# Two relational graph layers, gathered in slots of four chunks in place of eight

## The chip, the cores and the metric

The kernel runs on one core of one Trainium2 chip. The metric is the time of the whole kernel on the device, in microseconds (us), lower is better. Engines: PE (TensorE, matrix products), DVE (VectorE), ACT (ScalarE), POOL (GpSimd, here the engine that issues gathers), SP (which issues plain DMAs). They run side by side and wait for each other by semaphores.

## What is computed

3125 nodes with 128 features, 100,000 edges sorted by destination, each with one of 8 relations. A graph convolution of two layers, a layer norm, then a relational part of two layers and a second layer norm:

```
def _rgcn_layer(x, W, SW, b, src, dst, rel):
    xt = jnp.einsum('nd,rde->rne', x, W)
    msg = xt[rel, src]
    agg = jax.ops.segment_sum(msg, dst, num_segments=x.shape[0])
    return jax.nn.relu(agg + x @ SW + b)
x = _layernorm(x + _L0_gnn_ref(x, ...))
x = _layernorm(x + _L1_gnn_ref(x, ...))   # two _rgcn_layer
```

The change touches the two relational layers alone, which the kernel numbers 2 and 3.

## The kernel before

Nodes are padded to NP = 3200 (25 tiles of 128). Edges are taken in chunks of 128, 782 in all. With the sorted destinations, chunk c reaches a window of WIN = 64 nodes that begins BACK = 32 nodes ahead of node 4c.

**Two ways to add up.** Each relational layer splits its nodes. The first nodes (1280 in layer 2, 1536 in layer 3) are *summed*: counts of edges by destination, relation and source ("halves" of 32 nodes, 1.6 MB each, built on PE in strips, L1297, from one-hots that DVE makes, L1809 and L1812, copied by ACT, L929) are multiplied by the features, split into three bf16 parts (L1385). One pair of halves takes 75 products; two pairs make a quad of 128 nodes, which `end_quad` multiplies by the relation weights (L1432, L1435). DVE (layer 2, L1917) or ACT (layer 3, L982) copies the sums of a pair from PSUM before that. The other nodes are *gathered*: the rows x·W of all nodes and relations lie in a table in DRAM (`table_rel`), POOL gathers the 128 rows of a chunk by an indirect DMA (L798), and PE multiplies them by a one-hot of destinations (`add_message`, L1408) which DVE makes for a whole batch (`node_onehots`, L1925).

**Slots.** PE's program in a relational layer is written as a row of slots, and `Gathers` sets their number: one for each batch of CH = 8 chunks, 59 in layer 2 and 51 in layer 3. A slot holds a share of the counts and sum products (`Made` cuts 384 steps over all slots but the last two of layer 2; `spread_sums` deals the 1725 products of layer 3 over all but the last three) and the messages of its batch, spread evenly among the products. Ahead of the first message of a batch PE waits for the batch's one-hots (`node_hots`) and for all its rows (`got_rows`). At a slot's end PE does what came due in it: `end_quad`, and in layer 2 the turning of a finished tile and its rows for layer 3's table (`turn_tile`, L1445; `row_products`, L1449; the second row product follows in the middle of the next slot). ACT and DVE do their parts (L1004, L1007, L1014; L1933, L1938, L1944) in the same slots, SP stores the rows (L651), halves (L668) and results. One tile is begun in a slot at most (`tile_order`). In layer 3 a final norm follows by `turn_final` (L1517), ACT's L989 or L997, DVE's L1954 and L1961 to L1969.

**Buffers and pace.** Gathered rows have GATHERS = 6 buffers of 8 chunks (three in the memory of `node_id`, three in that of `acc`), one-hots ONEHOTS = 4 of 8 chunks. POOL may gather batch n once batch n - 6 was used, and is also paced: ahead of each two gathers of slot n it waits until PE has come as far in slot n - AHEAD (AHEAD = 2), in layer 2 by counted strips (`rstrip_counted`), in layer 3 by quarters of a slot's products (`quarter_summed`, four to a slot).

Of the kernel before, what the change touches and what calls it, by code (L numbers as in the profile page):

```python
# [4 lines left out]
N_NODES, D, R, CTX = 3125, 128, 8, 64  # L5
# [6 lines left out]
CH = BATCH // P  # L12
# [3 lines left out]
CHUNKS = -(-E // P)  # L16
# [46 lines left out]
BACK, WIN = 32, 64  # L63
GATHERS, ONEHOTS, HOTS, RINGS = 6, 4, 3, 4

AHEAD = 2
QUAD = 4 * HALF
# [31 lines left out]
class Gathers:  # L99
# [5 lines left out]
    def __init__(self, first_node):  # L105
        self.first_node = first_node
        self.first = (first_node - BACK) // PER_CHUNK + 1
        self.slots = -(-(CHUNKS - self.first) // CH)
        whole = NP - LAST_BLOCK
        self.blocks = [(a, min(a + BANK, whole)) for a in range(first_node, whole, BANK)] + [(whole, NP)]  # L110
        self.in_slot = [[] for _ in range(self.slots)]
        self.end_slot = []
        self.batch_end = {}
        slot = 0
        for q, (a, b) in enumerate(self.blocks):
            for c in range(self.first, CHUNKS):
                base = PER_CHUNK * c - BACK
                if base + WIN > a and base < b:
                    batch = (c - self.first) // CH
                    slot = max(slot, batch)  # L120
                    self.batch_end[batch] = (slot, len(self.in_slot[slot]))
                    self.in_slot[slot].append((c, max(a, base), min(b, base + WIN), q))
            self.end_slot.append(slot)
            slot = min(slot + 1, self.slots - 1)

    def chunks(self, batch):
        first = self.first + CH * batch
        return first, min(CH, CHUNKS - first)

# [88 lines left out]
def gnn_kernel(nc, x, src, dst, rel, ctx_in, W1, b1, W2, b2, Wg, bg, Wb, w1, sl1, rb1, w2, sl2, rb2, out):  # L218
# [8 lines left out]
    with ExitStack() as stack:  # L227
# [6 lines left out]
        raw = sb("raw", [P, 8, BATCH])  # L234
# [17 lines left out]
        node_id = sb("node_id", [P, NP + W])  # L252
# [18 lines left out]
        acc = sb("acc", [P, NP + W])  # L271
# [16 lines left out]
        def carve(at, n):  # L288
# [18 lines left out]
        half_pairs = [blocks[:, u, :].rearrange("p (h n) -> p h n", h=2) for u in range(2)]  # L307
        nodehot = raw[:, 5:7, :].rearrange("p a (u c w) -> p (a u) c w", u=2, c=CH)
        rest3 = raw[:, 7, 0:2 * P].rearrange("p (u n) -> p u n", u=2)
# [8 lines left out]
            + [edge_mem[:, 2 * EDGE_COLS:2 * EDGE_COLS + NP // 2].bitcast(bf16)]  # L318
        got = [m[:, u * CH * D:(u + 1) * CH * D].rearrange("p (c f) -> p c f", c=CH) for m in (node_id, acc) for u in range(3)]
        wg1, wg2, ws1, ws2 = (sb(n, [P, D]) for n in ("wg1", "wg2", "ws1", "ws2"))  # L320
# [51 lines left out]
        half_summed, half_copied, quarter_summed = sem("half_summed"), sem("half_copied"), sem("quarter_summed")  # L372
# [111 lines left out]
        for layer in (2, 3):  # L484
            for n in range(gathers[layer].slots):
                u = (first_batch[layer] + n) % GATHERS
# [237 lines left out]
        def _(pool):  # L724
# [42 lines left out]
            def rest_of(slow):  # L767
# [8 lines left out]
                if not slow:  # L776
                    pool.wait_ge(edges_copied, CH)
                    for layer in (2, 3):
# [5 lines left out]
                        for n in range(gathers[layer].slots):  # L784
# [5 lines left out]
                            for j in range(chunks):  # L790
# [4 lines left out]
                                if layer == 3 and j % 2 == 0 and n >= AHEAD and sums3[n - AHEAD]:  # L795
                                    pool.wait_ge(quarter_summed, 4 * (n - AHEAD) + j // 2 + 1)
                                    pool.nop(nofuse=True)
# [289 lines left out]
        def _(pe):  # L1087
# [119 lines left out]
            def rest_of(slow):  # L1207
# [184 lines left out]
                def add_message(layer, s, i):  # L1392
                    own = gathers[layer]
                    c, a, b, q = own.in_slot[s][i]
                    batch, j = (c - own.first) // CH, (c - own.first) % CH
                    m = first_batch[layer] + batch
                    start_, end_ = own.blocks[q]
                    if c == next(chunk for t in own.in_slot for chunk, _, _, block_ in t if block_ == q):
                        if first_block[layer] + q:
                            pe.wait_ge(gather_out, first_block[layer] + q)  # L1400
                        nc.tensor.matmul(ps[:, GATHER_BANK, 0:end_ - start_], layer_self[layer][:, :], layer_in[layer][:, start_:end_],
                                         start=True, stop=False)
                    if i == 0 or (own.in_slot[s][i - 1][0] - own.first) // CH != batch:
                        pe.wait_ge(node_hots, m + 1)
                        pe.wait_ge(got_rows[m % GATHERS], rows_until[m])
# [666 lines left out]
```

## Time and profile before

| | |
|---|---|
| median of 3 runs | 1827.04 us (1826.1 to 1836.43) |
| profiled execution | 1842.08 us |
| its span, first to last instruction | 1840.2 us |
| PE busy | 1562.5 us (85%) |
| DVE busy | 779.7 us (42%) |
| ACT busy | 520.8 us (28%) |
| POOL busy | 917.4 us (50%) |
| mean granted clock of PE | 0.949 of full |
| chain that ended last | PE 66%, DVE 14% |

PE's clock has two levels, 1.2 and 2.4 GHz; a granted clock of 0.83 in a stretch is a mean over both. The relational layers begin where POOL's first gather does, at 462 us, and layer 3's first gather is at 1231 us. Busy times overlap between engines, so what counts is where PE stands still, and what it then waits for.

### The profile page before, as it was taken

How to read it: one execution, taken by the hardware profiler on the slowest of the kernel's cores; microseconds unless marked ns; L12 is line 12 of the kernel's file. 1: busy time of each engine (PE TensorE's matmuls, PEld its weight loads, DVE VectorE, ACT ScalarE, POOL GpSimd, SP SyncE). 2: the span in 40 equal slices, each digit the busy share in tenths (PEclk: the TensorE clock that was granted, in tenths of full speed). 3: DMA queues.
4: the chain of work that ended last, by engine and by line, in shares of the span. 5: the costliest groups of instructions: out<-in, count | busy, mean ns of one | idle time of the engine just before them, and what ended most of it. 6: DMA issues, size and time to landing. Idle time of an engine off the chain costs nothing.

```text
span 1840.2 us, 25393 instructions
## 1 busy us (share of the span) xinstructions
PE 1562.5 (85%) x9744; PEld 949.8 (52%) x9744; DVE 779.7 (42%) x2390; ACT 520.8 (28%) x749; POOL 917.4 (50%) x931
## 2 busy tenths in 40 slices
PE   1379989998578889988899787898888998889986
PEld 1365554444355556555565455554555655556545
DVE  7999961337345555555465654530010010001102
ACT  0464520015234435444354543420000000000000
POOL 6500000000566566666666665646666666666665
PEclk9999999999789899999899998998999999989988
DMA  4312331534443444544455443325555355555441
GB/s 124 103 73 90 127 162 72 195 129 185 155 141 134 151 156 165 189 163 159 151 182 179 157 157 122 113 82 189 186 192 189 123 190 188 190 189 178 172 148 47
DMA packets 67473, 275.85 MB, mean 150 GB/s; under 512 B 19988, under 2 KB 25854, under 8 KB 54676
## 3 DMA queue, kind: packets, MB, share of 16 engines
q1 hardware_dynamic: 37940, 213.87, 30.1%
q0 software_dynamic: 29408, 60.29, 12.1%
q8 instruction: 81, 1.33, 0.3%
q14 instruction: 44, 0.36, 0.1%
HBM read 153.70 MB, written 120.38 MB: 149 GB/s over the span
## 4 chain that ended last, share of the span: by engine, by line
PE 66%; DVE 14%; another core or an unknown queue 6%; issue 6%; DMA 3%; POOL 2%; ACT 2%; POOLq 0%; DVEq 0%; ACTq 0%
PE ps L1385 34%; DVE hot_mem L1667 8%; PE ps L1408 8%; PE ps L1263 7%; PE ps L1297 7%; PE ps L1449 2%; PE ps L1435 2%; PE ps L1306 2%; ACT blocks L929 2%; DMA node_id<-table_rel,edges 1%; POOL node_id L798 1%; DMA acc<-table_rel,edges 1%; DVE hot_mem L1812 1%; POOL acc L798 1%
## 5 line engine op out<-in xcount | busy, mean ns | idle before, releaser
L798 POOL DMA_INDIRECT node_id<-table_rel,edges x445 | 439.0, 987 | 608.0 <-DMA table_rel<-node_id 358.3
L798 POOL DMA_INDIRECT acc<-table_rel,edges x429 | 419.3, 977 | 257.5 <-issue 113.2
L1385 PE MATMUL ps<-blocks,raw 128*128 128x512 f16 x1500 | 456.5, 393 | 15.5 <-DVE xn L1917 12.5
L929 ACT ACTIVATE blocks<-ps 128x800 f16<-128x800 f32 x384 | 315.6, 836 | 342.3 <-PE ps L1297 200.0
L1385 PE MATMUL ps<-blocks,dinv 128*128 128x512 f16 x1200 | 399.3, 395 | 13.5 <-issue 12.8
L1809 DVE TENSOR_SCALAR hot_mem<-cell_h,rel_cols 128x128 f16<-128x128 f16 x768 | 165.6, 268 | 265.9 <-PE ps L1297 152.9
L1297 PE MATMUL ps<-hot_mem 128*128 128x400 f16 x768 | 198.8, 344 | 68.0 <-ACT blocks L929 47.5
L1408 PEld LDWEIGHTS ps<-raw,node_id 128*128 128x128 f32 x996 | 193.8, 200 | 97.7 <-issue 38.9
L1385 PE MATMUL ps<-blocks,edges 128*128 128x512 f16 x600 | 236.8, 395 | 7.9 <-issue 7.6
L1408 PEld LDWEIGHTS ps<-raw,acc 128*128 128x128 f32 x962 | 183.7, 197 | 85.4 <-issue 31.0
L1812 DVE TENSOR_SCALAR hot_mem<-cell_h,rel_cols 128x400 f16<-128x400 f16 x768 | 224.8, 333 | 0.0
L1385 PEld LDWEIGHTS ps<-blocks,raw 128*128 128x128 bf16 x1500 | 164.4, 116 | 110.7 <-issue 35.1
L1408 PE MATMUL ps<-raw,node_id 128*128 128x64 f32 (+14 forms) x996 | 168.0, 252 | 26.4 <-DMA node_id<-table_rel,edges 19.1
L1385 PEld LDWEIGHTS ps<-blocks,dinv 128*128 128x128 bf16 x1200 | 132.4, 115 | 105.2 <-issue 35.1
L1408 PE MATMUL ps<-raw,acc 128*128 128x64 f32 (+13 forms) x962 | 159.0, 250 | 16.7 <-DMA acc<-table_rel,edges 9.1
L1667 DVE TENSOR_TENSOR hot_mem<-hot_mem,edges 128x2048 f16<-128x2048 f16 x200 | 164.0, 885 | 10.7 <-remote 8.2
L1954 DVE TENSOR_TENSOR tin<-tin,xT 128x128 f32<-128x128 f32 (+3 forms) x16 | 5.9, 366 | 347.7 <-ACT tin L989 267.1
L1297 PEld LDWEIGHTS ps<-hot_mem 128*128 128x128 f16 x768 | 73.3, 108 | 152.1 <-ACT blocks L929 75.5
L1119 PE MATMUL ps<-hot_mem 128*128 128x50 f16 x1600 | 65.1, 195 | 57.2 <-DVE hot_mem L1667 41.6
L854 ACT ACTIVATE blocks<-ps 128x800 f16<-128x800 f32 x100 | 83.0, 837 | 73.2 <-PE ps L1119 61.8
L1119 PEld LDWEIGHTS ps<-hot_mem 128*128 128x128 f16 x1600 | 57.6, 103 | 88.2 <-ACT blocks L854 42.3
L982 ACT ACTIVATE raw<-ps 128x512 f32<-128x512 f32 x24 | 25.3, 1055 | 266.3 <-remote 155.6
(183 smaller groups left out, 1296.2 us busy)
## 6 DMA issues: line engine op xcount, KB each, us to landing
rcounts<-blocks SPq DMA_DIRECT2D x44, 1600.0 KB
blocks<-rcounts SPq DMA_DIRECT2D x44, 1600.0 KB
counts<-blocks SPq DMA_DIRECT2D x6, 3200.0 KB, 11.0
blocks<-counts SPq DMA_DIRECT2D x5, 3200.0 KB, 10.5
table_rel<-node_id SPq DMA_DIRECT2D x50, 256.0 KB, 2.1
table_rel<-xn SPq DMA_DIRECT2D x50, 256.0 KB
node_id<-table_rel,edges POOLq DMA_INDIRECT x445
acc<-table_rel,edges POOLq DMA_INDIRECT x429
```

Source lines behind the costliest of these rows:

```text
L798: nc.gpsimd.indirect_dma_start(got[m % GATHERS][:, j, :], None, tables_rel[layer - 2], bass.IndirectOffsetOnAxis(ap=row_i[:, first + j:fir ...
L854: nc.scalar.activation(block_of(b)[:, :, at:at + 2 * PAIR * CH].rearrange("p t (u n) -> p t u n", u=2), ps[:, 2 * (h % 2):2 * (h % 2) + 2, ...
L929: nc.scalar.activation(to.rearrange("p t (b m) -> p t b m", b=2), ps[:, strip_bank(k):strip_bank(k) + 2, 0:RCELLS].rearrange("p b (m t) -> ...
L1119: last = nc.tensor.matmul(ps[:, 2 * (h % 2) + c // CH, c % CH * GKEYS:(c % CH + 1) * GKEYS], low_hot[:, h % HOT_RING, c // 2, :, c % 2], c ...
L1263: nc.tensor.matmul(total, part, buffer_of(i)[:, t * n:(t + 1) * n], start=first, stop=False)
L1297: last = nc.tensor.matmul(ps[:, strip_bank(k) + c, 0:RCELLS], rlow_hot[:, k % HOTS, c, :], rcell_hot[:, k % HOTS, c, :], start=True, stop= ...
L1306: nc.tensor.matmul(ps[:, q % FAST_BANKS, :], xT[:, t * P:(t + 1) * P], wr1[:, 4 * h:4 * h + 4, :].rearrange("p r f -> p (r f)"), start=Tru ...
L1385: last = nc.tensor.matmul(ps[:, bank, 0:2 * HCOLS], part, half_pairs[u % 2][:, :, t * HCOLS:(t + 1) * HCOLS], start=(k == 0), stop=(k == T ...
L1408: last = nc.tensor.matmul(ps[:, GATHER_BANK, a - start_:b - start_], got[m % GATHERS][:, j, :], nodehot[:, m % ONEHOTS, j, a - base:b - ba ...
L1667: last = nc.vector.tensor_tensor(hot[:, u, :, :, :], each_h[:, 0:n, :].unsqueeze(1).to_broadcast([P, CH, n, 2]), keys.unsqueeze(2).to_broa ...
L1809: nc.vector.tensor_scalar(rlow_hot[:, u, c, :], cell_h[:, 0:P], rel_cols[:, 0, first + c:first + c + 1], 0.0, ALU.subtract, ALU.is_equal)
L1812: last = nc.vector.tensor_scalar(rcell_hot[:, u, c, :], cell_h[:, :], rel_cols[:, 1, first + c:first + c + 1], 0.0, ALU.subtract, ALU.is_e ...
```

## The change

A new constant GCH = 4 takes the place of CH = 8 in the relational layers. Batches of gathers, their buffers, one-hots and waits for rows are of four chunks. Buffers double in number and halve in size, so memory is the same; AHEAD goes from 2 to 4 slots, the same 16 chunks. The number of slots doubles (59 to 118, 51 to 102), and with it everything that is dealt out by slots is cut anew.

```
-GATHERS, ONEHOTS, HOTS, RINGS = 6, 4, 3, 4
-
-AHEAD = 2
+GATHERS, ONEHOTS, HOTS, RINGS = 12, 8, 3, 4
+
+GCH = 4
+
+AHEAD = 4
...
-        self.slots = -(-(CHUNKS - self.first) // CH)
+        self.slots = -(-(CHUNKS - self.first) // GCH)
...
-                    batch = (c - self.first) // CH
+                    batch = (c - self.first) // GCH
...
-        first = self.first + CH * batch
-        return first, min(CH, CHUNKS - first)
+        first = self.first + GCH * batch
+        return first, min(GCH, CHUNKS - first)
...
-        nodehot = raw[:, 5:7, :].rearrange("p a (u c w) -> p (a u) c w", u=2, c=CH)
+        nodehot = raw[:, 5:7, :].rearrange("p a (u c w) -> p (a u) c w", u=ONEHOTS // 2, c=GCH)
...
-        got = [m[:, u * CH * D:(u + 1) * CH * D].rearrange("p (c f) -> p c f", c=CH) for m in (node_id, acc) for u in range(3)]
+        got = [m[:, u * GCH * D:(u + 1) * GCH * D].rearrange("p (c f) -> p c f", c=GCH) for m in (node_id, acc) for u in range(GATHERS // 2)]
...
-                                    pool.wait_ge(quarter_summed, 4 * (n - AHEAD) + j // 2 + 1)
+                                    pool.wait_ge(quarter_summed, 4 * (n - AHEAD) + 4 * j // GCH + 1)
...
-                    batch, j = (c - own.first) // CH, (c - own.first) % CH
+                    batch, j = (c - own.first) // GCH, (c - own.first) % GCH
...
-                    if i == 0 or (own.in_slot[s][i - 1][0] - own.first) // CH != batch:
+                    if i == 0 or (own.in_slot[s][i - 1][0] - own.first) // GCH != batch:
```

The changed file has two lines more, so its L1387 is L1385 of before, and so on.

PE's program at the first message of layer 2, before (L1385 sum products, L1401 the block's own term, L1408 messages, L1297 counts; the words in brackets are the semaphores waited for):

```order
L1385 MATMUL ps<-blocks,raw 128x512 x4
L1401 MATMUL ps<-xT,ws 128x512
L1408 MATMUL ps<-raw,node_id 128x4 [waits got_rows0,node_hots]
...
L1408 MATMUL ps<-raw,node_id 128x32
...
L1385 MATMUL ps<-blocks,raw 128x512 x4
L1408 MATMUL ps<-raw,node_id 128x36 [waits got_rows1,node_hots]
```

And after:

```order
L1387 MATMUL ps<-blocks,raw 128x512 x3
L1403 MATMUL ps<-xT,ws 128x512
L1410 MATMUL ps<-raw,node_id 128x4 [waits got_rows0,node_hots]
...
L1410 MATMUL ps<-raw,node_id 128x16
...
L1410 MATMUL ps<-raw,node_id 128x20 [waits got_rows1,node_hots]
```

The first wait now asks for four chunks' rows, and the fifth message has a wait of its own, where before the ninth had.

PE's program around the fourth quad of layer 2 (L1432 and L1435 are the quad), before, from the last messages of its second pair:

```order
L1385 MATMUL ps<-blocks,raw 128x512
L1297 MATMUL ps<-hot_mem 128x400 [waits rhots_ready,rstrip_copied]
L1297 MATMUL ps<-hot_mem 128x400
L1297 MATMUL ps<-hot_mem 128x400 [waits rhots_ready,rstrip_copied]
L1297 MATMUL ps<-hot_mem 128x400
L1385 MATMUL ps<-blocks,raw 128x512 [waits half_copied,rstrip_copied,low_ready]
...
L1408 MATMUL ps<-raw,acc 128x64
L1432 MATMUL ps<-xT,ws 128x128 [waits quad_out,half_copied,tile_rest]
L1435 MATMUL ps<-xn,wr 128x128 x8
```

And after:

```order
L1387 MATMUL ps<-blocks,raw 128x512 x3
L1410 MATMUL ps<-raw,acc 128x64
L1434 MATMUL ps<-xT,ws 128x128 [waits quad_out,half_copied,tile_rest]
L1437 MATMUL ps<-xn,wr 128x128 x8
L1299 MATMUL ps<-hot_mem 128x400 [waits rhots_ready,rstrip_copied]
L1299 MATMUL ps<-hot_mem 128x400
L1299 MATMUL ps<-hot_mem 128x400 [waits rhots_ready,rstrip_copied]
L1299 MATMUL ps<-hot_mem 128x400
L1387 MATMUL ps<-blocks,raw 128x512 [waits half_copied,rstrip_copied,low_ready]
```

The quad moved from several steps behind the end of its pair to right behind the pair's last product. This is so for 9 of the 10 quads of layer 2; before it was so for 3.

PE's program at the end of layer 3, from the last sum product on, before (L1517 turns the finished tiles for the final norm):

```order
L1408 MATMUL ps<-raw,acc 128x64 [waits got_rows5,node_hots]
L1408 MATMUL ps<-raw,acc 128x64 x7
L1432 MATMUL ps<-tin,ws 128x128 [waits quad_out,half_copied]
L1435 MATMUL ps<-raw,wr 128x128 x8
L1408 MATMUL ps<-raw,node_id 128x64 [waits got_rows0,node_hots]
L1408 MATMUL ps<-raw,node_id 128x64 x7
L1517 MATMUL ps<-ident,tin 128x128 [waits group_normed,sum_ready]
L1408 MATMUL ps<-raw,node_id 128x64 [waits got_rows1,node_hots]
L1408 MATMUL ps<-raw,node_id 128x64 x4
```

And after:

```order
L1410 MATMUL ps<-raw,node_id 128x64 [waits got_rows1,node_hots]
L1410 MATMUL ps<-raw,node_id 128x64 x3
L1434 MATMUL ps<-tin,ws 128x128 [waits quad_out,half_copied]
L1437 MATMUL ps<-raw,wr 128x128 x8
L1410 MATMUL ps<-raw,node_id 128x64 [waits got_rows2,node_hots]
L1410 MATMUL ps<-raw,node_id 128x64 x3
L1519 MATMUL ps<-ident,tin 128x128 [waits group_normed,sum_ready]
L1410 MATMUL ps<-raw,node_id 128x64 [waits got_rows3,node_hots]
```

Of 21 messages behind the last sum product, 9 are left there; the other 12 moved in among the products.

## Rows read from the trace of the kernel before

**Rows 1.** Page, head: the span.

```profile
span 1840.2 us, 25393 instructions
```

**Rows 2.** Windows of layers 2 and 3: PE, PEld, DVE, ACT, POOL busy; clock, DMA, GB/s.

```profile
475.00:1215.00 740.00, 640.24 (x3539) 400.11 (x3539) 395.72 (x1593) 326.64 (x445) 460.01 (x460) 0.94 0.44 150
1226.00:1840.00 614.00, 540.19 (x2951) 332.07 (x2948) 59.66 (x161) 37.27 (x58) 388.42 (x405) 0.93 0.47 166
```

**Rows 3.** Waits of PE, 475 to 1200: us in total, times, longest.

```profile
PE ps L1385 <- DVE xn L1917: 12.5, 11, 2.6
PE ps L1432 <- DVE xn L1917: 6.1, 1, 6.1
```

**Rows 4.** Start of layer 2: PE and POOL in time (start, us), then the chain.

```profile
474.83 0.56 PE L1408 MATMUL ps<-raw,node_id 128*128 128x4 f32 x2 [7.91 <-DMA node_id<-table_rel,edges]
...
467.14 0.94 POOL L798 DMA_INDIRECT node_id<-table_rel,edges  x1 [0.30 <-issue]
...
472.13 2.57 DMA node_id<-table_rel,edges
```

**Rows 5.** PE in time, layer 3: waits for rows amid the layer.

```profile
1305.65 0.41 PE L1408 MATMUL ps<-raw,acc 128*128 128x64 f32 x2 [3.69 <-DMA acc<-table_rel,edges]
...
1377.44 0.41 PE L1408 MATMUL ps<-raw,acc 128*128 128x64 f32 x2 [1.83 <-DMA acc<-table_rel,edges]
...
1423.63 0.66 PE L1408 MATMUL ps<-raw,node_id 128*128 128x64 f32 x2 [4.37 <-DMA node_id<-table_rel,edges]
...
1553.88 0.41 PE L1408 MATMUL ps<-raw,node_id 128*128 128x64 f32 x2 [2.05 <-DMA node_id<-table_rel,edges]
...
1576.31 0.66 PE L1408 MATMUL ps<-raw,acc 128*128 128x64 f32 x2 [3.63 <-DMA acc<-table_rel,edges]
```

**Rows 6.** Chain ahead of the first of these waits.

```profile
1298.99 6.19 DMA acc<-table_rel,edges
```

**Rows 7.** Windows behind three of these waits: PE busy, granted clock, DMA, GB/s.

```profile
1305.00:1315.00 10.00, 9.35 (x44) 0.83 0.18 49
...
1423.00:1433.00 10.00, 9.37 (x38) 0.67 0.39 129
...
1576.00:1586.00 10.00, 9.07 (x42) 0.83 0.13 35
```

**Rows 8.** Waits of POOL for PE in layer 3, 1230 to 1830.

```profile
POOL node_id L798 <- PE ps L1385: 33.6, 20, 3.3
...
POOL acc L798 <- PE ps L1385: 22.7, 16, 2.9
```

**Rows 9.** DVE groups by form, 475 to 1230: busy, mean ns, idle before.

```profile
L1925 DVE TENSOR_TENSOR raw<-cell_h,edges 128x512 f32<-128x512 f16 x58 | 39.4, 680 | 0.0
L1917 DVE COPY xn<-ps 128x512 f32<-128x512 f32 x20 | 20.4, 1022 | 25.5 <-remote 12.9 <-issue 6.6 <-PE ps L1385 6.0
...
L1925 DVE TENSOR_TENSOR raw<-cell_h,edges 128x320 f32<-128x320 f16 x1 | 0.5, 483 | 0.0
```

**Rows 10.** End of layer 3, in time.

```profile
1816.50 1.06 ACT L982 ACTIVATE raw<-ps 128x512 f32<-128x512 f32 x1 [6.87 <-PE ps L1385]
...
1818.53 1.95 PE L1435 MATMUL ps<-raw,wr 128*128 128x128 f32 x16
...
1823.42 1.97 PE L1408 MATMUL ps<-raw,node_id 128*128 128x64 f32 x16 [2.94 <-DMA node_id<-table_rel,edges]
...
1827.01 0.95 POOL L798 DMA_INDIRECT node_id<-table_rel,edges  x1 [0.30 <-issue]
1827.43 0.37 ACT L989 ACTIVATE tin<-ps,cols 128x128 f32<-128x128 f32 x1 [9.88 <-remote]
...
1830.28 2.37 PE L1408 MATMUL ps<-raw,node_id 128*128 128x64 f32 x10 [1.63 <-DMA node_id<-table_rel,edges]
...
1833.75 0.69 PE L1517 MATMUL ps<-ident,tin 128*128 128x128 f32 x2 [1.11 <-DVE tin L1954]
```

**Rows 11.** Page, DMA issues: KB each, median us from issue to landing.

```profile
table_rel<-node_id SPq DMA_DIRECT2D x50, 256.0 KB, 2.1
```

## The prediction

> **What bounds the kernel now.** I read the page's head first: the span is 1840.2 us [rows 1], the whole profiled execution 1842.08, 15 above the median of 1827.04. The sum below is made against 1842.08, and its difference is then taken off the median. Windows over the two relational layers come next [rows 2]: PE is busy for 640 of 740 us in layer 2 and for 540 of 614 in layer 3, at a granted clock of 0.94 and 0.93. DVE, ACT and POOL are far below, so PE's own work sets the pace, and what a change of slots can win is PE's standing still and what that does to its clock. What PE stands still for differs by layer. In layer 2 it waits for DVE's copy of a pair's sums [rows 3], for ACT's copies of counts, and once for gathered rows, at the very start: 7.91 us [rows 4]. In layer 3 it waits for gathered rows five times amid the layer, for 3.69, 1.83, 4.37, 2.05 and 3.63 us [rows 5], 15.6 together, and twice more at the end, for 2.94 and 1.63 us [rows 10].
>
> **Why the batch size decides these waits.** PE needs all eight chunks' rows at the first message of a batch, though it uses them one by one over a slot of some 12 us (614 us over 51 slots). POOL issues a gather each 1.25 us: four of them lie between 467.14 and 472.13, where the eighth begins [rows 4]. The rows land 2.57 us after that start at the layer's start [rows 4], and 6.19 us after it amid layer 3, where SP loads pairs of halves beside them [rows 6]. So with batches of four the rows asked for at the start of an old slot are there 4 x 1.25 = 5.0 us earlier, and those of chunks five to eight are asked for half a slot later, about 6 us, which is more than the 5.0 that they lag.
>
> **Layer 2's start.** With four chunks PE goes on at 467.14 + 2.57 + 0.14 = 469.9 in place of 474.83: 5.0 us saved. The fifth message, with the next wait, comes three strips later, after its rows landed at about 474.7. Bounds: 3 (something else is late next) and 7.9 (the whole wait).
>
> **The five waits of layer 3.** Each is below 5.0 us, so by itself each goes: 15.6 us. The limit is POOL: 405 gathers x 1.25 = 506 us against a layer of 614, and POOL stood waiting for PE for 33.6 + 22.7 us [rows 8]. It has room, but PE, which no longer stops, comes nearer to POOL's last landed row each time. From first chunk needed to farthest chunk allowed there were 8 chunks of play, now 12; I give back one wait of the size of the larger ones, 5 us. Bounds of the term: 5 and 15.6 won, of which I take 10.6.
>
> **The clock behind them.** Behind three of these waits the granted clock over ten us is 0.83, 0.67 and 0.83 [rows 7], that is the lower level of 1.2 GHz for part of it, after PE had stood still: 1.7 + 3.3 + 1.7 = 6.7 us lost. Bounds 0 and 6.7; I take half, 3.3, since low stretches also come where no such wait stands ahead. The Trainium skill (TensorE: Matmul & The Clock Gate, Part 1: The HAM clock gate) has the array throttled by default and released by activity; the trace agrees with these three windows, and by that rule alone all 6.7 us would come back.
>
> **The end.** The last products end at 1816.5, where ACT's L982 begins [rows 10], and the span ends 23.7 us later. Behind them lie 21 messages, and POOL's last gather only begins at 1827.01, since eight to a batch and three slots without products leave the last 13 gathers to run at 1.25 us each behind PE's last quarters. After the change the last gather waits only for the first quarter of slot 97 of 99 that hold products, so all rows have landed by the last product. Twelve messages move ahead of it: 1.97 us for eight [rows 10], 3.0 for twelve. Then: copy of the last pair (1.06) and the quad (1.95 and its L1432) end 3.4 us behind the last product, ACT, DVE and the turn of that tile take until 5.1, the last message, ACT and DVE (1.1 between 1832.65 and 1833.75) and 0.7 for DVE's norm of the tile before until 7.2, and from the last turn at 1833.75 to the end are 6.45: 13.6. With the 3.0 that makes 16.6 against 23.7, 7.1 won. One thing speaks against it: ACT's L989 began at 1827.43, though the quad's records end at 1820.48; if these 7 us are real and come back, nothing is won. Bounds 0 and 7.1; I take 4.
>
> **What it costs.** (a) One-hots: DVE makes 110 more of half the size. From 680 ns at 512 elements and 483 at 320 [rows 9] the slope is 1.03 ns and the fixed part 155 ns, so 110 x 0.155 = 17 us more on DVE, spread over a DVE that is busy for 396 of 740 and 60 of 614 us [rows 2]: hidden. If that cover were gone in layer 2, 59 of them, 9 us, would show. The Trainium skill (VectorE: DVE Perf Modes, The TRN2 errata) states a fixed extra cost for each instruction with SBUF operands, about 150 cycles measured; that is a rule against this change, the rows agree with it in size, and it would move the sum only if DVE were the bound. (b) 110 more waits for rows on PE and 110 more on POOL. At batch starts whose rows are there, the trace shows no idle time, on POOL none above the usual 0.30 us: nothing, at most 0.1 us each, 11. (c) Quads in layer 2: six more come right behind their pair's last product and so meet DVE's copy of 1.02 us [rows 9] at full length. Until now PE met that copy two strips of counts later, for 12.5 / 11 = 1.1 us [rows 3]; afterwards that later wait is gone. I take 1.5 against 1.1: 0.4 x 6 = 2.4. Bounds: 0, and the 6.1 us that one quad in this position waited [rows 3], 5 x 6 = 30. (d) Between the layers, 10 messages in place of 26 passes' worth cover the turn of the last tile and ACT's and DVE's copies: 1 us, bounds 0 and 2 (two copies of 1.02). (e) Tiles in a row now come each half slot. Their rows' stores land in 2.1 us [rows 11] and the ring of four stages gives them two slots, about 12 us: hidden. If a 1.6 MB store of a half lies ahead in the queue it adds up to 10.7 us (at the mean of 150 GB/s [rows 2]), 12.8 in all, so that such a tile would wait 1 us at most.
>
> **Sum.** -5.0 - 10.6 - 3.3 - 4 + 2.4 + 1 = -19.5: 1842.1 becomes 1822.6, and the median 1827.04 becomes about 1807.5, 1.1% less.
>
> **The rivals.**
> 1. *The waits come back elsewhere.* POOL's pace of 10.0 us for eight gathers is close to PE's for a slot at the full clock (PE busy 540 us over 51 slots is 10.6). For it: POOL's 506 us in 614. Against it: POOL itself waited 56 us. Then only 5 of the 15.6 us and no clock are won: -5 - 5 - 2 + 3.4 = -8.6, 1818. Chance 0.27.
> 2. *More of the clock comes back.* All 6.7 us, the full 15.6, the 7.1 at the end: -5 - 15.6 - 6.7 - 7.1 + 3.4 = -31, 1796. It needs that PE stands still only at these places. Chance 0.13.
> 3. *Slower: quads wait for DVE.* DVE serves strips' one-hots, pairs' copies and tiles in program order; a quad right behind its pair waits for whatever stands ahead of the copy, as one did for 6.1 us. Six times 5 us more, with the gains of the forecast but (c): -21.9 + 30 = +8, 1835. It decides from about 3.7 us more for each quad. Against it: of the three quads in that position only one shows such a wait [rows 3]. If tiles at half spacing are drawn in too it can pass 1845. Chance 0.10.
> 4. *Nothing moves.* The rows' waits are an accident of the profiled execution, and the unprofiled runs have other bounds. Chance 0.08, 1827.
>
> **The numbers.** Forecast 0.42 for 1800 to 1814; its own range 1800 to 1814. The whole range reaches over the first two rivals and part of the third: 1793 to 1828. A difference of 1% (18.3 us) is about what a measurement of this kernel can tell from none: faster is below 1808.8. Of the forecast a little over half lies there, all of rival 2 and little of rival 1: 0.23 + 0.13 + 0.04 = 0.40; slower, above 1845.3, only the far end of rival 3: 0.05; the same 0.55.
>
> **What would show it.** In the changed kernel's profile: PE's first wait for rows in layer 2 near 3 us in place of 7.9; no wait for rows above 1 us amid layer 3, or at most one; the clock behind them above 0.9; POOL's last gather before PE's last sum product, and 17 to 24 us from that product to the end; PE's waits for L1917's copy (L1919 there) at quads (L1434) near 1 us each, 10 in all. The prediction is wrong if rows' waits of the same sum stand at other places in layer 3 (rival 1), if L1434's waits sum to over 20 us (rival 3), or if the busy time of PE in layer 2 stretches with waits for ACT that were not there.

## The result: 1.6% slower where it was first measured, the same elsewhere

The changed kernel took 1860.4 us (median of 4 runs, 1852.5 to 1866.4) beside 1831.3 us (4 runs, 1826.1 to 1836.4): a ratio of 1.0156, 95% interval [1.0097, 1.0215]. The forecast was 1807.5 and its range ended at 1828; the direction was wrong.

One thing has to be said ahead of everything else, since without it no number below can be read. The chips ran this program in one of two conditions, which hold for all kernels of a job. In the **long** one the kernel before takes some 1830 us (the first measurement and two later jobs), in the **short** one 1625 us (five jobs on five chips; the two later long jobs ran on one of these five). A job is a set of kernels run side by side on one chip, and all comparisons are within a job. Where the kernel before takes 1625 us, the changed kernel takes 0.9998 times that. One execution of the kernel before, in a long job, took 5117 us and is left out.

| time against the kernel before | short | long |
|---|---|---|
| batches of four, slots of eight | 0.9937, 0.9926, 0.9945 | 0.9999 [0.9967, 1.0030] |
| batches of four, slots of four in layer 3 only | 0.9937 [0.9924, 0.9951] | 1.0048 [1.0003, 1.0092] |
| batches of four, slots of four in layer 2 only | 0.9991 [0.9982, 1.0000] | |
| the change (four and four) | 0.9998 [0.9989, 1.0007] | 1.0156 [1.0097, 1.0215] |
| batches of eight, slots of four | 1.0086 [1.0073, 1.0100] | |

### The profile page after: what moved, and what is told of

It is laid out like the page before. It is cut to its first block, busy times and chain, and to the rows that moved or that the text cites. A ratio compares the mean times of both kernels' runs of the same rounds, so it can differ in the third digit from the quotient of the medians.

```text
span 1850.4 us, 25734 instructions
## 1 busy us (share of the span) xinstructions
PE 1572.6 (85%) x9744; PEld 957.8 (52%) x9744; DVE 783.2 (42%) x2500; ACT 519.4 (28%) x749; POOL 922.3 (50%) x931
## 4 chain that ended last, share of the span: by engine, by line
PE 67%; DVE 13%; issue 9%; another core or an unknown queue 6%; ACT 4%; DMA 1%; POOL 0%; DVEq 0%; ACTq 0%; POOLq 0%
PE ps L1387 34%; PE ps L1299 8%; PE ps L1410 8%; DVE hot_mem L1669 8%; PE ps L1265 8%; ACT blocks L931 3%; PE ps L1437 2%; PE ps L1451 2%; PE ps L1308 2%; DVE hot_mem L1814 1%; PE ps L1434 0%; DVE xn L1919 0%; DVE hot_mem L1811 0%; PE ps L1267 0%
## 5 line engine op out<-in xcount | busy, mean ns | idle before, releaser
L800 POOL DMA_INDIRECT acc<-table_rel,edges x429 | 424.6, 990 | 245.5 <-issue 112.6
L1387 PE MATMUL ps<-blocks,raw 128*128 128x512 f16 x1500 | 450.7, 393 | 5.4 <-DVE xn L1919 4.1
L1387 PE MATMUL ps<-blocks,dinv 128*128 128x512 f16 x1200 | 401.9, 396 | 31.5 <-issue 30.7
L931 ACT ACTIVATE blocks<-ps 128x800 f16<-128x800 f32 x384 | 313.7, 837 | 342.8 <-PE ps L1299 213.6
L1387 PE MATMUL ps<-blocks,edges 128*128 128x512 f16 x600 | 237.8, 396 | 13.0 <-issue 12.7
L1387 PEld LDWEIGHTS ps<-blocks,raw 128*128 128x128 bf16 x1500 | 162.0, 114 | 102.9 <-issue 22.9
L1387 PEld LDWEIGHTS ps<-blocks,dinv 128*128 128x128 bf16 x1200 | 132.7, 115 | 123.7 <-issue 54.7
L1927 DVE TENSOR_TENSOR raw<-cell_h,edges 128x256 f32<-128x256 f16 x220 | 85.8, 415 | 51.5 <-remote 33.3
```

What stands on the lines that cost most here:

```text
L800: nc.gpsimd.indirect_dma_start(got[m % GATHERS][:, j, :], None, tables_rel[layer - 2], bass.IndirectOffsetOnAxis(ap=row_i[:, first + j:fir ...
L931: nc.scalar.activation(to.rearrange("p t (b m) -> p t b m", b=2), ps[:, strip_bank(k):strip_bank(k) + 2, 0:RCELLS].rearrange("p b (m t) -> ...
L1387: last = nc.tensor.matmul(ps[:, bank, 0:2 * HCOLS], part, half_pairs[u % 2][:, :, t * HCOLS:(t + 1) * HCOLS], start=(k == 0), stop=(k == T ...
L1927: nc.vector.tensor_tensor(nodehot[:, m % ONEHOTS, 0:chunks, :], cell_h[:, 0:WIN].unsqueeze(1).to_broadcast([P, chunks, WIN]), spread(chunk ...
```

## The profile after

Of the changed kernel, long condition. First the two layers (window, its length, busy time of PE, PEld, DVE, ACT, POOL, granted clock, DMA share, GB/s), which answer to [rows 2]:

```profile
475.00:1215.00 740.00, 639.12 (x3516) 401.55 (x3515) 394.99 (x1647) 321.78 (x442) 465.54 (x459) 0.94 0.43 150
1230.00:1850.00 620.00, 543.55 (x2950) 334.38 (x2948) 63.41 (x212) 37.54 (x58) 387.74 (x405) 0.93 0.47 164
```

Nothing has become busier and the clock is what it was; layer 2 as a window can't be told from before. What PE waits for in layer 3 (1200 to 1850; us in total, times, longest), the changed kernel:

```profile
PE ps L1387 <- issue: 43.4, 59, 2.1
PE ps L1410 <- issue: 15.5, 15, 1.7
PE ps L1434 <- issue: 3.1, 2, 2.1
PE ps L1519 <- DVE tin L1956: 2.9, 2, 1.7
PE ps L1410 <- DVE raw L1927: 2.3, 1, 2.3
```

and the kernel before, same window:

```profile
PE ps L1385 <- issue: 20.5, 34, 1.7
PE ps L1408 <- issue: 14.6, 17, 1.9
PE ps L1408 <- DMA node_id<-table_rel,edges: 11.2, 5, 4.4
PE ps L1408 <- DMA acc<-table_rel,edges: 9.1, 3, 3.7
PE ps L1435 <- issue: 5.1, 8, 1.1
```

The waits for gathered rows, 20.3 us at the foot of the lower list, are all gone in the upper one, as forecast. But "issue" (PE stands still and nothing in the profile releases it) rose by 23 us at the sum products, so that PE's waits in layer 3 together are no smaller than before. That is what the forecast didn't have. Whether these 23 us are what makes the change slower is another question: 16 of them also stand in a version that is not slower (the last experiment). Such a stop in the timeline of the changed kernel (start, us, engine, line; in brackets the idle time before):

```profile
1289.31 0.39 PE L1410 MATMUL ps<-raw,node_id 128*128 128x64 f32 x2
1291.58 0.59 PE L1387 MATMUL ps<-blocks,dinv 128*128 128x512 f16 x2 [1.89 <-issue]
1292.01 0.46 PE L1387 MATMUL ps<-blocks,edges 128*128 128x512 f16 x1
1294.38 0.59 PE L1387 MATMUL ps<-blocks,dinv 128*128 128x512 f16 x1 [1.91 <-issue]
1294.76 0.58 PE L1410 MATMUL ps<-raw,node_id 128*128 128x64 f32 x2
1296.48 0.59 PE L1387 MATMUL ps<-blocks,dinv 128*128 128x512 f16 x1 [1.14 <-issue]
```

No semaphore is waited for at these products. Windows around this stop and a later one (columns as above):

```profile
1289.00:1302.00 13.00, 7.95 (x26) 4.06 (x24) 0.00 (x0) 0.00 (x0) 7.22 (x9) 0.62 0.14 38
...
1574.00:1586.00 12.00, 7.94 (x27) 3.48 (x26) 0.00 (x0) 1.04 (x1) 6.62 (x7) 0.72 0.22 51
```

The granted clock falls to 0.62 and 0.72, as it did behind the waits for rows in [rows 7]; in the ten us ahead of the first window (1279 to 1289) it was 1.00. So the low clock that the forecast put down to the waits for rows comes with stops of the other kind too, and removing the rows' waits didn't remove it.

Layer 2, 475 to 1200, the changed kernel:

```profile
PE ps L1299 <- ACT blocks L931: 64.4, 40, 5.2
PE ps L1434 <- issue: 15.8, 8, 3.7
...
PE ps L1387 <- DVE xn L1919: 4.1, 7, 1.1
PE ps L1434 <- DVE xn L1919: 2.6, 1, 2.6
```

and the kernel before, same window:

```profile
PE ps L1297 <- ACT blocks L929: 46.3, 31, 4.5
```

Against [rows 3] the waits at the next pair's product fell from 12.5 to 4.1 us, and those at the quads rose from 8.7 (6.1 for DVE and 2.6 put down to issue) to 18.4, so that in this trace the two nearly cancel. The experiment with late quads below shows, for the short condition, that "issue" at L1434 is the wait for DVE's copy, though the profile doesn't name it. The largest wait of layer 2 is the one for ACT's copies of counts. The forecast named it and gave it no price, and it is 18 us longer after the change. That can't be put down to the slots: with slots of eight, in the last experiment, it is 60 us.

The layer's start:

```profile
465.74 0.95 POOL L800 DMA_INDIRECT node_id<-table_rel,edges  x1 [0.31 <-issue]
...
471.13 0.56 PE L1410 MATMUL ps<-raw,node_id 128*128 128x4 f32 x2 [5.82 <-DMA node_id<-table_rel,edges]
```

The fourth gather starts 1.4 us earlier than in [rows 4] and PE goes on 3.7 us earlier, but the wait only shrinks from 7.91 to 5.82: the rows take 5.2 us to land, not the 2.57 of the eighth.

The end:

```profile
1837.37 0.38 PE L1387 MATMUL ps<-blocks,edges 128*128 128x512 f16 x1
...
1837.79 1.05 ACT L984 ACTIVATE raw<-ps 128x512 f32<-128x512 f32 x1 [21.90 <-PE ps L1387]
...
1841.20 0.37 ACT L991 ACTIVATE tin<-ps,cols 128x128 f32<-128x128 f32 x1 [2.37 <-PE ps L1437]
...
1844.19 0.44 PE L1519 MATMUL ps<-ident,tin 128*128 128x128 f32 x2 [1.67 <-DVE tin L1956]
```

From ACT's last copy of sums to the end of the span are 12.6 us, where they were 23.7 [rows 10]: 11.1 less. The 7 us in which L989 stood in [rows 10] did come back. And yet the last copy comes 21.3 us later, at 1837.8 in place of 1816.5.

## Experiments

**Dealing and batches apart.** A kernel in which the slot (what PE's, DVE's, SP's and POOL's programs are dealt by) and the batch (rows, buffers, one-hots, waits) have sizes of their own; with 4 and 4 it is the changed kernel instruction by instruction, with 8 and 8 the one before.

```
+SLOT = {2: 8, 3: 8}
-AHEAD = 4
+AHEAD = {2: 16 // SLOT[2], 3: 16 // SLOT[3]}
...
-                    slot = max(slot, batch)
+                    slot = max(slot, (c - self.first) // slot_chunks)
...
-                            node_onehots(2, s + 1)
+                            for n in gathers[2].of_slot(s + 1):
+                                node_onehots(2, n)
```

Batches of four, slots of eight:

> Undoes the dealing alone: batches, buffers, one-hots and waits for rows stay at four chunks, the slots (and with them the counts, products, quads, tiles and POOL's pace) are those of the kernel before, of eight. Theory A (the finer dealing costs the time): the five waits for rows are gone, the rest is as before, so 1810 to 1825 us. Theory B (the 110 more waits and one-hots, with their separate wait instructions on PE, cost it): about 1850 to 1860 us as in the changed kernel, and PE's idle time put down to issue in layer 3 is above 60 us. Theory C (PE that no longer stops for rows stops for something else, whatever the dealing): 1827 to 1835 us, no row waits and more idle time put down to issue than the kernel before.

Batches of eight, slots of four:

> The dealing alone: slots of four as in the changed kernel, but batches, buffers and one-hots of eight chunks over two slots, with one wait a batch as before. Theory A: the loss is all here, 1855 to 1870 us (1860 and the row waits on top, the shorter end off). Theory B: no loss, 1815 to 1830 us since the shorter end stays. Theory C: 1827 to 1840 us.

Slots of four in layer 3, and in layer 2, alone:

> Batches of four in both layers; slots of eight in layer 2, of four in layer 3. Theory A with the loss in layer 3 (17 us between its first and last product in the profiles): 1850 us or a little more; A with the loss in layer 2: 1825. Theory B: 1855. Theory C: 1830.

> Batches of four in both layers; slots of four in layer 2, of eight in layer 3. Theory A with the loss in layer 3: 1820 to 1835 us (the 8 us that layer 2 lost in the profiles, less the row waits); A with the loss in layer 2: 1850. Theory B: 1855. Theory C: 1830.

The job met the short condition: 1624.8 us before, and 1614.3, 1639.9, 1614.9 and 1623.1. Smaller batches alone win 0.6%; slots of four in layer 2 give that back (8.8 us between the first and the fourth); in layer 3 they change nothing; and slots of four without the smaller batches lose 0.9%. So theory A holds for layer 2, B falls (the batches carry the 110 more waits and are faster), C falls here.

**The two kernels again, and the waits alone.**

> The kernel before, unchanged, for its trace beside the other runs of this job. In the four runs so far this kernel took 1624.8 us, 202 us less than the 1827.0 of the first measurement, at a granted clock of 0.99 in place of 0.949. Two theories of that: D, these were other conditions of the chip, and then the waits that the first trace puts down to issue on PE (some 40 us in layer 3) and to remote on ACT and DVE (some 90 us) are absent or below 10 us where the kernel takes 1625 us, and there again where it takes over 1800; E, the waits are there in both, and only the clock differs. Ratio 1.00.

> The changed kernel, unchanged. By the two runs with slots of four in one layer each (0.9937 for layer 3, 0.9991 for layer 2, against 0.9937 with slots of eight in both) it should take 0.999 of the kernel before, 1623 us, if the conditions are those of these runs. If it is 1.010 to 1.021 here too, the two layers' dealing adds up to more than its parts. If the chip is as at first (the kernel before at over 1800 us), 1.010 to 1.021 again.

```
+                    if j == 4 and i and (own.in_slot[s][i - 1][0] - own.first) // CH == batch:
+                        pe.wait_ge(node_hots, m + 1)
+                        pe.wait_ge(got_rows[m % GATHERS], rows_until[m])
```

> The kernel before with a second pair of waits (one-hots and rows, both satisfied long ago) ahead of the fifth message of each batch: the wait instructions of the changed kernel alone, nothing dealt anew. Theory A and C: 1.000. Theory B (the wait instructions themselves cost PE time): 1.005 or more where the chip is calm, 1.01 or more where it is as at first.

The short condition again: 1625.8, 1624.4 and 1623.8 us, ratios of 1.000, 0.9998 and 0.9996. The waits cost nothing there. PE's waits over the whole relational part, kernel before in this job:

```profile
PE ps L1408 <- DMA node_id<-table_rel,edges: 19.8, 6, 7.9
PE ps L1385 <- DVE xn L1917: 7.8, 13, 1.2
PE ps L1408 <- DMA acc<-table_rel,edges: 6.4, 4, 2.3
...
PE ps L1432 <- issue: 2.6, 3, 1.0
```

and the changed one:

```profile
PE ps L1410 <- DMA node_id<-table_rel,edges: 18.1, 11, 5.8
PE ps L1434 <- issue: 8.4, 9, 1.0
PE ps L1387 <- DVE xn L1919: 5.3, 10, 1.1
PE ps L1410 <- DMA acc<-table_rel,edges: 4.4, 5, 2.0
```

Theory D holds: in the relational layers "issue" is absent but for the quads. "Remote" (a releaser on another core or an unknown queue) is absent on every engine as well. In the first trace, long condition, it stood ahead of ACT's copies of counts, of DVE's one-hots for the counts and of POOL's gathers (85 us in both layers, 45 of them in layer 3):

```profile
ACT blocks L929 <- remote: 93.1, 29, 6.8
DVE hot_mem L1809 <- remote: 83.1, 25, 6.8
```

So in the long condition all of these engines stop, not PE alone, and with them PE waits for ACT's copies of counts: 46.3 us there, 1.3 us here.

Waits for rows are hardly fewer with batches of four: 22.5 us in place of 26.2. POOL tells why (its waits in layer 3, kernel before, same job):

```profile
POOL node_id L798 <- issue: 55.4, 180, 0.6
...
POOL acc L798 <- PE ps L1385: 8.9, 28, 0.7
POOL node_id L798 <- PE ps L1385: 8.0, 25, 0.7
```

28 waits for 8.9 us are little more than the usual 0.30 us between two gathers: in layer 3 of the short condition POOL practically never waits for PE, where it waited 56 us in the long one [rows 8]. Layer 3 is then as long as POOL's 405 gathers. Its first and last, before:

```profile
1099.55 1.47 POOL L798 DMA_INDIRECT acc<-table_rel,edges  x1 [15.63 <-DMA table_rel<-xn]
...
1611.56 0.94 POOL L798 DMA_INDIRECT node_id<-table_rel,edges  x1 [0.30 <-issue]
```

and in the changed kernel, same job:

```profile
1100.92 0.94 POOL L800 DMA_INDIRECT acc<-table_rel,edges  x1 [23.17 <-DMA table_rel<-xn]
...
1609.26 0.94 POOL L800 DMA_INDIRECT node_id<-table_rel,edges  x1 [0.30 <-issue]
```

512.0 and 508.3 us for 404 steps, 1.27 and 1.26 us each, and 13.3 and 12.0 us behind the last one. PE waits for rows because POOL is no faster, so smaller batches move these waits and hardly shrink them. With slots of eight and batches of four the first gather of layer 3 is at 1091.7, 7.9 us earlier than before and 9.3 earlier than after: what happens ahead of that gather, in layer 2, is where most of the short condition's time is won or lost.

**Quads away from their pair's end.**

```
-... if begin[2 * i + 2] - 1 in r) for i in range(USED // 4)]
+... if begin[2 * i + 2] - 1 in r) + (i < 9) for i in range(USED // 4)]
```

> The changed kernel with nine of layer 2's ten quads one slot of four later, so that they no longer stand right behind their pair's last product. Under the conditions of the last two jobs (kernel before at 1625 us) PE's waits at the first product of a quad (L1434) fall from 8.4 us in 9 to at most 3, and those at the next pair's first product rise by at most 2; the rest of the kernel has the waits that it had. If this step of the dealing is what layer 2 pays, the time is 4 us below the changed kernel's, a ratio of 0.997; if it is hidden elsewhere, 0.9998 as before. If the conditions are the first ones (over 1800 us), the ratio falls from 1.016 to between 1.010 and 1.013.

> Batches of four with the slots of eight once more, on whatever chip this is. Where the kernel before takes 1625 us: 0.9937 again, which says that 0.6% is the gain of smaller batches and not of that chip. Where it takes over 1800 us: theory A (the finer dealing is what costs there) 0.985 to 0.995; theory C (a PE that doesn't stop for rows stops for its own instructions instead) 1.00 or above.

Short condition: 0.9958 [0.9944, 0.9971] and 0.9926 [0.9913, 0.9940]. Of the late quads, PE's waits in layer 2 (475 to 1090):

```profile
PE ps L1387 <- DVE xn L1919: 6.8, 16, 0.5
...
PE ps L1434 <- issue: 1.0, 1, 1.0
```

The changed kernel had 9.3 us at the quads (8.4 put down to issue, 0.9 to DVE); now it is 1.0, and the next pair's products take 1.5 more. Against 0.9998 for the change, in another job, this is 6.5 us, so quads right behind their pair are about three quarters of the 8.8 us that slots of four cost in layer 2 of the short condition. The rest is not told apart, and in the long condition this version was not run.

**Is it enough that PE sets the pace?** The same extra work in three kernels: a count product of each strip is issued twice, and behind every fourth product of layer 3 one more goes to a bank that nobody reads.

```
-                    for c in range(2):
+                    for c in (0, 0, 1):
...
+                    if layer == 3 and u >= 2 and k % 4 == 3:
+                        nc.tensor.matmul(ps[:, SUM_BANK, 0:2 * HCOLS], part, half_pairs[u % 2][:, :, t * HCOLS:(t + 1) * HCOLS],
+                                         start=True, stop=True)
```

> The kernel before with extra work on PE spread evenly, so that PE sets the pace of both layers as in the first measurement although the chip is as in the last jobs: the first of the two count products of each strip of layers 2's counts is issued twice, and behind every fourth product of layer 3 (from its third pair on) one more of the same size goes to a PSUM bank that nobody reads. 384 and some 400 products of 0.28 us: 1625 + 107 + 50 to 110 = 1780 to 1840 us. POOL's gathers then no longer set the pace of layer 3: it waits for PE for over 30 us there.

> The same extra work in the changed kernel. Theory P (slots of four cost the 1.0 to 2.1% wherever PE sets the pace): 1.010 to 1.021 times the kernel before with the same extra work. Theory S (what they lose to are the stops of PE's own instruction stream, which only the first measurement shows): no slower than it, and since the forecast's gains (row waits, end) hold where PE sets the pace, 0.990 to 1.000 of it.

> The same extra work with batches of four and slots of eight. Both theories: below the kernel before with the same extra work, 0.990 to 0.995 of it. P: 1.5 to 2.5% below the changed kernel with it; S: within 0.7% of that.

1748.9, 1741.1 and 1740.6 us, short condition: the change is then 0.45% faster than the kernel before, and the slots make no difference. The 780 extra products made the kernel longer by 0.16 us each (124 / 780) and not by 0.28, so the times are below the expectation; in part they fill what were waits for rows. But PE sets the pace: beside the layer's start PE waits for rows for 7.9 us in the kernel before and for none in the changed one, and POOL waits for PE (kernel before with the extra work, from 1180 us on):

```profile
POOL node_id L798 <- PE ps L1385: 38.0, 32, 2.8
POOL acc L798 <- PE ps L1385: 34.6, 29, 2.8
```

Theory P falls: a layer paced by PE is not, by itself, what the change loses in. What is left is what the long condition has beside that: PE's own stops, and those of ACT, DVE and POOL. No run takes these apart.

**Stops put in by hand, and the long condition met again.** Bursts of 20 products at every twelfth strip and behind every 70th sum product.

> The kernel before with PE held up in bursts as the first trace shows it: in layer 2 at every twelfth strip of counts its first product is issued 20 times more, in layer 3 behind every 70th sum product (from the third pair on) 20 products of the same size go to a PSUM bank that nobody reads: 5 to 6 us each time, 31 and 24 times. 1625 + 170 in layer 2, and in layer 3 + 50 to 130: 1800 to 1880 us.

> The same bursts in the changed kernel. Theory S as put in numbers: if stops of PE in bursts are what slots of four can't take, 1.008 to 1.021 times the kernel before with the same bursts. Theory T (the length and spacing of PE's stops is not it; something else of the first conditions is, such as stops of the other engines' streams): 0.990 to 1.002 of it.

> The same bursts with batches of four and slots of eight. Both theories: 0.988 to 0.998 of the kernel before with the same bursts.

The job met the long condition (kernel before, without bursts, 1826.4 us, on a chip that had given 1625 before), so the bursts came on top of the stops that were there, and the experiment is not what it was meant to be: it can't decide between S and T. It still orders the kernels: 1888.9, 1907.3 and 1891.8 us. The changed kernel is 1.0% slower (18.4 us; its four runs are 1901.5 to 1916.0, those of the kernel before 1884.4 to 1895.0), batches of four with slots of eight are 0.2% slower, within the noise. So slots of four cost 0.8% here, the one comparison of the two within a job of the long condition. An odd thing: 1069 more products, an estimated 170 us at the 0.16 us of the evenly spread ones, made the kernel only 62 us longer. The stops shrank: "issue" in layer 3 fell to 8.5 us at the sum products where bursts were put in, all of PE's waits in the two layers from some 180 us in the first trace to some 90, and the granted clock of the runs rose from 0.948 to 0.957 without bursts to 0.977 to 0.983 with them.

Kernel before with bursts, 1200 us on:

```profile
PE ps L1385 <- issue: 8.5, 15, 1.1
```

**The faster version once more, and the layers in the long condition.**

> Batches of four with slots of eight. Where the kernel before takes over 1800 us: if the dealing by four is what costs there (A), 0.990 to 1.003; if the batches, their waits and their one-hots are (B), 1.010 to 1.021 like the changed kernel; if PE merely trades its row waits for stops of its own (C), 0.998 to 1.005. Where it takes 1625 us: 0.993 once more.

> As for the third time: over 1800 us, A: 0.990 to 1.003, B: 1.010 to 1.021; at 1625 us: 0.993 to 0.995.

> Batches of four, slots of eight in layer 2 and of four in layer 3. Over 1800 us: 1.008 or more if the loss is in layer 3's dealing (the first traces put 17 of the 22 us up to the last product there), 0.995 to 1.003 if it is in layer 2's. At 1625 us: 0.994 once more.

The third time was short: 1615.8 beside 1625.3 us, 0.9945. The fourth was long: 1827.6 us (10 runs) beside 1832.2 (14 runs), 0.9999, and slots of four in layer 3 1843.4 us (6 runs), 1.0048 [1.0003, 1.0092]. So A holds here as well: with the batches of the change but the slots of before there is no loss. B falls in the long condition too. Slots of four in layer 3 cost 0.5%, which the interval only just tells from nothing: two of the six runs are at 1829 and 1831 us, the other four at 1843 to 1846. The 1.1% that is left to the change's 1.0156 would be layer 2's dealing; it is a difference of two ratios from two jobs, and with their intervals anything from 0.3 to 1.8%. The traces of the long condition agree for layer 3 and can't settle layer 2 (us between the first and the last sum product of a layer, and from the last one to the end of the span):

| long condition, profiled execution | layer 2 | layer 3 | end |
|---|---|---|---|
| before | 749.5 | 589.8 | 24.1 |
| batches of four, slots of eight | 730.1 | 589.1 | 25.1 |
| batches of four, slots of four in layer 3 only | 743.2 | 615.5 | 13.2 |
| the change | 755.8 | 607.2 | 13.0 |

In layer 3 slots of four stretch the products by 17 to 26 us and shorten the end by 11 to 12. In layer 2 the second and third row have the same program and still differ by 13 us, more than the change differs from before.

C fits the batches, by one trace of each kernel: PE's waits in layer 3 of the fourth run, with slots of eight

```profile
PE ps L1395 <- issue: 36.3, 50, 1.9
PE ps L1413 <- ACT tin L1007: 9.8, 2, 8.8
PE ps L1421 <- issue: 9.8, 17, 1.5
PE ps L1448 <- issue: 5.6, 9, 1.1
PE ps L1421 <- DMA node_id<-table_rel,edges: 5.0, 2, 3.8
```

hold 15.3 us less of waits for rows than before, 15.8 us more of "issue" at the sum products and 10 us of waits for ACT that were not there, and nothing is won in time.

## Why the forecast was wrong, point by point

- **Layer 2's start** (5.0 forecast, bounds 3 and 7.9): 2.1 us won. The mechanism was right, the size was not: the step took the landing time of the eighth gather (2.57) for the fourth, whose rows landed in 5.2 us. A store of 1.6 MB was issued 2.8 us before that gather; that it delays the rows wasn't tested.
- **Five waits of layer 3** (10.6): they vanished from the profile to the last one, and the time didn't. This is the step that failed. It treated named idle time on PE as time of the kernel, with POOL as the only thing that could give it back. In the long condition, by the traces, it came back as PE's own stops and waits for ACT (the batches alone: 0.9999), in the short condition layer 3 is POOL's gathers from end to end. Rival 1 had the outcome (waits come back elsewhere) but named POOL, and looked for rows.
- **The clock behind them** (3.3): 0.949 before, 0.948 after. Nothing. Low windows stand behind PE's own stops as well as behind waits for rows.
- **The end** (4, bounds 0 and 7.1): 11.1 us less from the last copy of sums to the end, of which 3.0 are the twelve messages that moved ahead of it: 8.1 won there, twice the term and above its bound. But the stretch of products ahead of it grew by 17 us, which no term had. In the short condition it is not a gain at all: batches of four in both, slots of four in layer 3 or of eight, 1614.9 and 1614.3 us, since there the end is set by POOL's last gather, and dealing the products over 99 slots of four in place of 48 of eight only shifts PE's last product towards it.
- **Quads in layer 2** (+2.4, bounds 0 and 30): +9.7 us in the profile at L1434 in the long condition, +5.8 in the short. In the short condition the mechanism, rival 3's, was the right one and its usual price too low: the next pair's product was expected to lose its wait in exchange, and it only fell from 7.8 to 5.3 us; moving the quads gave back 6.5. In the long condition the exchange did take place in the trace (12.5 to 4.1 us, 1.3 net of the 9.7), and what the quads cost there was not measured. The forecast also counted one wait at the quads of the kernel before, the 6.1 us; its trace has three more at L1432, 3.6 us, under "issue". The forecast named "L1434's waits over 20 us" as its refutation; they were 18.4 up to 1200 us and 21.5 over both layers, so that the sign appeared only just, and not with the time that rival 3 gave it.
- **Seam** (+1) and tiles (0): between the last product of layer 2 and the first of layer 3 the changed kernel's lag fell by 1.0 us, where 1 more was forecast, and PE's waits at tiles (L1447, L1451) are below 1 us each.
- **One-hots and waits for rows** (0): right. A one-hot of 256 elements took 415 ns (155 + 256 x 1.03 = 419 by [rows 9]), and PE waited for one once, 2.3 us. The Trainium skill (VectorE: DVE Perf Modes, The TRN2 errata) has a fixed cost per instruction, measured as about 150 cycles for the whole fixed term and not on top of one; at the 0.96 GHz it gives for DVE that is an estimated 156 ns, and the 155 ns of [rows 9] agree. It did not show in the time: DVE was busy for 395 of 740 us and 63 of 620. The 110 more waits: 0.9996 [0.9986, 1.0005] by themselves, in the short condition.
- **What was missing.** "Issue" on PE (46 us in layer 3 before) was read as part of PE's work, and in layer 2 PE's waits for ACT's copies (46 us) were left unpriced. These are the biggest idle times of the long condition, and both grew as the waits for rows went. They are not by themselves the change's loss: the version with slots of eight has much of the same growth and no loss.

By sum: forecast -19.5, measured +29. Of the mechanisms tried, the short condition gives batches of four -0.6% (10 us), layer 2's dealing +0.5% to 0.6%, layer 3's 0. The long one gives 0, +1.1% by subtraction across jobs, and +0.5%.

**What stays open.** Why slots of four cost more in the long condition (0.8 to 1.6% against 0.6%), the loss that the first measurement shows. The changed kernel's PE stream there stops in more places (59 at the sum products, 34 before, 50 with slots of eight), but the profile names no releaser, the extra waits cost nothing where they could be tried, and a layer paced by PE isn't it. Whether it is PE's stops or those of ACT, DVE and POOL that the slots can't take was not tried apart. That the waits are harmless in the long condition is shown only together with the batches. Layer 2's share there was never measured alone, the late quads were not run there, and the two profiled executions (1842.1 and 1852.5 us) differ by 10 us where the medians differ by 29, so the traces hold a third of the loss at most.

The version that beats both in the short condition has batches of four and slots of eight: 0.55 to 0.74% faster in three jobs. In the long condition it is level with the kernel before.

## What to carry to other kernels

- Before pricing a named wait, ask what bounds the stretch once it is gone: look for an engine that never waits longer than its usual gap (POOL here), and for idle time that nothing releases. Either takes the gain.
- When one constant sets both the size of a buffer and the grain of the dealing, change them apart. In the short condition small batches were good and small slots were not, mostly because a reduction moved to sit right behind the copy it needs; together they were nothing. In the long condition only the loss was left.
- Measure the kernel before in the same job. The loss of this result belongs to a condition of the chip in which the kernel takes 12% longer. And where engines stop for no named reason, one trace is one sample: two with the same program of layer 2 differed by 13 us in it.

## What the runs showed of the hardware

- The same kernel on the same chip took 1625 us in one job and 1827 to 1832 in two others, at a mean granted clock of 0.982 to 0.988 against 0.948 to 0.957. Only the relational layers differ much: the first sum product starts at 456 to 458 us in the short condition and at 458 to 468 in the long one. In the long condition PE stops at the sum products of layer 3 for up to 2.1 us at a time, several times in a row (4 to 5 us idle within 12 or 13), and the clock is granted at 0.62 and 0.72 over the 13 and 12 us around two such places. ACT, DVE and POOL have stops of their own (the "remote" waits, up to 6.8 us ahead of ACT's copies of counts and DVE's one-hots for them, and 3.7 ahead of gathers) that the short condition lacks. The Trainium skill (TensorE: Matmul & The Clock Gate, Part 1: The HAM clock gate) has the clock fall for want of activity; the trace agrees as to the order, stop first and low clock behind it, but says nothing of what makes the stop.
- Extra products on PE partly fill these stops: an estimated 170 us of them (1069 at the 0.16 us measured in the short condition), in bursts, cost 62, and the granted clock rose from about 0.95 to 0.98.
- POOL's indirect gathers go out at 1.26 us each without a break over 508 us when nothing holds them.
